# Cross attention whose stacked keys and queries go from SBUF to SBUF in 24 transfers per half batch

## What is computed

```python
qp = q @ Wq.T
kv = latent_kv @ Wkv_expand.T
k, v = jnp.split(kv, 2, axis=-1)
scores = jnp.einsum('bhqd,bhkd->bhqk', qh, kh) * inv_sqrt_d
scores = jnp.where(causal, scores, jnp.finfo(scores.dtype).min)
attn = jax.nn.softmax(scores, axis=-1)
out = jnp.einsum('bhqk,bhkd->bhqd', attn, vh)
return out.transpose(0, 2, 1, 3).reshape(b, sq, H) @ Wout.T
...
x = _layernorm(x + _L0_attn_ref(...), axis=-1)    # a gated convolution
x = _layernorm(x + _L0_xattn_ref(...), axis=-1)   # this part
x = _layernorm(x + _L0_ffn_ref(...), axis=-1)     # a mixture of experts
```

## Time and profile before

| | us |
|---|---|
| profiled execution, its own time | 1183.95 |
| its span | 1182.3 |
| median of the three runs | 1184.79 |
| PE busy | 1076.5 (91%) |
| DVE busy | 683.3 (58%) |
| ACT busy | 457.1 (39%) |
| POOL busy | 284.0 (24%) |

### The profile page before, as it was taken

One profiled execution on the slowest core, in us unless ns is written; L12 is line 12 of the kernel. 1 busy time (PEld: TensorE's weight loads), 2 busy tenths in 40 slices (PEclk: granted clock), 3 DMA queues, 4 the chain that ended last, 5 costly groups with the idle time before them and its releaser, 6 DMA issues. The chain is left out here.

```text
span 1182.3 us, 19299 instructions
## 1 busy us (share of the span) xinstructions
PE 1076.5 (91%) x6850; PEld 910.4 (77%) x6850; DVE 683.3 (58%) x1517; ACT 457.1 (39%) x808; POOL 284.0 (24%) x370
## 2 busy tenths in 40 slices
PE   5999999998758999998868879999999999899996
PEld 4688888887547877886647669899999989777784
DVE  3746375562535666675344747777777767344475
ACT  4613334143324444453334235555555555221210
POOL 4510101006112232333234121111222110223030
PEclk9999999999968999998979889999999999899999
DMA  4402020303878778874243256766666775523141
GB/s 154 167 1 107 0 106 0 106 0 136 236 176 224 189 209 226 216 194 113 73 156 129 78 162 230 248 224 229 224 236 241 227 238 168 178 72 125 53 147 66
DMA packets 88818, 179.31 MB, mean 152 GB/s; under 512 B 8032, under 2 KB 33632, under 8 KB 87104
## 3 DMA queue, kind: packets, MB, share of 16 engines
q1 hardware_dynamic: 82096, 155.06, 42.1%
q0 software_dynamic: 6672, 23.60, 5.9%
HBM read 136.95 MB, written 41.42 MB: 151 GB/s over the span
## 5 line engine op out<-in xcount | busy, mean ns | idle before, releaser
L45 PE MATMUL e_ps_h<-e_x_lo,e_gu_hi 128*128 128x256 f32 (+1 forms) x552 | 155.9, 282 | 5.0 <-DVE e_x_lo L1812 5.0
L46 PE MATMUL e_ps_h<-e_x_hi,e_gu_lo 128*128 128x256 f32 (+1 forms) x552 | 153.8, 279 | 0.0
L47 PE MATMUL e_ps_h<-e_x_hi,e_gu_hi 128*128 128x256 f32 (+1 forms) x552 | 153.6, 278 | 0.0
L804 DVE CUSTOM_DVE_ANT_0 b_dump<-b_ps_s,b_mask 128x128 f32<-128x128 f32 (+1 forms) x256 | 80.1, 354 | 68.6 <-PE b_ps_s L990 67.4
L45 PE MATMUL a_ps_proj<-a_x_lo,arena 128*128 128x512 f32 x256 | 102.4, 400 | 14.9 <-DVE a_x_lo L295 12.1
L45 PEld LDWEIGHTS e_ps_h<-e_x_lo,e_gu_hi 128*128 128x128 f32 (+1 forms) x552 | 99.4, 180 | 6.3 <-DVE e_gu_lo L1816 5.2
L46 PE MATMUL a_ps_proj<-a_x_hi,arena 128*128 128x512 f32 x256 | 101.9, 398 | 0.0
L47 PE MATMUL a_ps_proj<-a_x_hi,arena 128*128 128x512 f32 x256 | 101.8, 398 | 0.0
L309 DVE SCALAR_TENSOR_TENSOR a_xc<-a_ps_proj,a_taps,a_xc 128x510 f32<-128x510 f32 (+2 forms) x96 | 71.6, 746 | 51.2 <-ACT a_xc L268 49.0
L46 PEld LDWEIGHTS e_ps_h<-e_x_hi,e_gu_lo 128*128 128x128 f32 (+1 forms) x552 | 99.5, 180 | 0.9
L47 PEld LDWEIGHTS e_ps_h<-e_x_hi,e_gu_hi 128*128 128x128 f32 (+1 forms) x552 | 99.4, 180 | 0.0
(11 more groups left out here) (306 smaller groups left out, 2699.7 us busy)
## 6 DMA issues: line engine op xcount, KB each, us to landing
f_gate_up_raw<-we_gate_up SPq DMA_DIRECT2D x88, 352.0 KB, 4.7
qk_split<-arena SPq DMA_DIRECT2D x32, 512.0 KB, 6.2
b_sk<-qk_split SPq DMA_DIRECT2D x48, 256.0 KB, 4.1
b_sq<-qk_split SPq DMA_DIRECT2D x48, 256.0 KB, 5.7
f_down_raw<-we_down SPq DMA_DIRECT2D x23, 512.0 KB, 6.7
y_slots<-f_y_tile SPq DMA_DIRECT2D x23, 512.0 KB, 2.8
f_x_next<-x SPq DMA_DIRECT2D x6, 1024.0 KB, 5.7
f_down_raw<-we_down SPq DMA_DIRECT2D x23, 192.0 KB, 6.7
```

The source lines that it names most:

```text
L45: pe.matmul(out, a_hi, b_lo, start=first, stop=False)
L46: pe.matmul(out, a_lo, b_hi, start=False, stop=False)
L47: return pe.matmul(out, a_hi, b_hi, start=False, stop=last)
L804: ins = dve.tensor_tensor_reduce(dump[:, n % 2, cols], ps_s[:, n % 2, cols], mask[:, cols], -1.0, 3e38, ALU.add, ALU.min, peak[:, u, k, i: ...
```

## The change

Three edits, all in `cross_attention`.

1. The DRAM tensor `qk_split`, its stores and the semaphore `split_stored` go. `load_direct` copies from `split` straight into the stacks: for each of three stacked parts and each of the four heads of a chunk one transfer of 32 partitions by 2 by 256 floats (64 KB), 12 for the keys and 12 for the queries of a half. In turns -2 and -1 SP issues the keys and ACT the queries, at fixed places between ACT's activations: batch 0 half 0 after the keys of its half 1; batch 0 half 1 after `fill(-1, 0, 1)`; batch 1 half 0 after `fill(-1, 1, 0)`; batch 1 half 1 after `peaks(0, 0)`, which now stands before the four normalizations. From turn 0 on SP issues both, keys and queries of a half together: half 0 after the residual load, half 1 after the peak rows of batch t+1. The keys' issue carries the wait for batch b-2's last below-peak product of the half. In `keys`, ACT's overwriting of `split` waits for the stack of the batch before instead of its store.
2. `attend` waits for the exponential of head 14 (bank 0 of `ps_x` is free then) and, chunk by chunk, for four more cuts.
3. `normalize` stands in slots (0, 1) and (0, 2), POOL's `rest` in (0, 3) and (0, 4).

```diff
+        def stack_count(b):
+            return 384 * (b + 1)
+        def load_direct(engine, into, parts, b, u):
+            for r, s in enumerate(parts):
+                for h in range(HC):
+                    engine.dma_start(into[r * HD:(r + 1) * HD, b % 2, u, h:UH:HC].bitcast(F32),
+                                     split[h * HD:(h + 1) * HD, u, s].bitcast(F32)).then_inc(stack_loaded[u], 16)
...
         @block.sync
+            def load_keys(b, u):
                 sp.wait_ge(xkq_lo_done, k_count(b, u))
...
                 if b >= 2:
                     sp.wait_ge(e_ready, order(b - 2, u, UH - 1) + 1)
+                load_direct(sp, sk, (KH, KL, KH), b, u)
+            def load_queries(b, u):
+                sp.wait_ge(xkq_lo_done, q_count(b, u))
+                load_direct(sp, sq, (QL, QH, QH), b, u)
...
-                if real(t + 2):
-                    store_k(t + 2, 0)
+                if t < 0:
+                    load_keys(t + 2, 0)
...
-                if real(t + 2):
-                    store_q(t + 2, 0)
-                    load_stack(t + 2, 0)
-                    store_k(t + 2, 1)
+                if t < 0:
+                    load_keys(t + 2, 1)
+                elif real(t + 2):
+                    load_keys(t + 2, 0)
+                    load_queries(t + 2, 0)
                 if real(t + 1):
                     load_peaks(t + 1, 0)
-                if real(t + 2):
-                    store_q(t + 2, 1)
-                    load_stack(t + 2, 1)
+                if t >= 0 and real(t + 2):
+                    load_keys(t + 2, 1)
+                    load_queries(t + 2, 1)
...
         @block.gpsimd
-                        if t and u == 0 and i in (4, 5):
-                            rest(t - 1, i - 4)
+                        if t and u == 0 and i in (3, 4):
+                            rest(t - 1, i - 3)
...
         @block.scalar
                 if b:
-                    act.wait_ge(split_stored, 32 * (2 * (b - 1) + u + 1))
+                    act.wait_ge(stack_loaded[u], stack_count(b - 1))
...
                 if t < 0:
-                    for u in range(2):
-                        for i in range(UH):
-                            fill(t, u, i)
+                    for i in range(UH):
+                        fill(t, 0, i)
+                        if t == -1 and i == 1:
+                            load_queries(0, 1)
+                    fill(t, 1, 0)
+                    load_queries(t + 2, 0)
+                    for i in range(1, UH):
+                        fill(t, 1, i)
                     if t == -1:
+                        peaks(0, 0)
+                        load_queries(1, 1)
                         act.wait_ge(ln_step, TILES + 7)
...
-                        peaks(0, 0)
...
         @block.vector
-                        if t and u == 0 and i in (2, 3):
-                            normalize(t - 1, i - 2)
+                        if t and u == 0 and i in (1, 2):
+                            normalize(t - 1, i - 1)
...
         @block.tensor
-                    pe.wait_ge(stack_loaded[u], 96 * (b + 1))
+                    pe.wait_ge(stack_loaded[u], stack_count(b))
...
             def attend(b):
-                pe.wait_ge(cut_done, HEADS * (b + 1))
+                pe.wait_ge(exp_done, HEADS * (b + 1) - 1)
                 for c in range(DC):
+                    pe.wait_ge(cut_done, HEADS * b + HC * (c + 1))
```

More of the change, by code:

```diff
@@ L384, in __init__, with cross_attention @@
                       (w_o[0], at[2][:, 0:h], at[3][:, 0:h]), (w_o[1], at[2][:, h:n], at[3][:, h:n])]
-def cross_attention(nc, x1_dram, ctx_t, weights, x2_dram, left_ln, ident, xt, c_raw, res, ln, spare, split_dram):
+def cross_attention(nc, x1_dram, ctx_t, weights, x2_dram, left_ln, ident, xt, c_raw, res, ln, spare):
     with ExitStack() as ctx:
@@ L447, in cross_attention @@
         xkq_lo_done = sem("xkq_lo_done")
-        split_stored = sem("split_stored")
         stack_loaded = pair("stack_loaded")
@@ L524, in _ @@
         def _(sp):
-            def store_k(b, u):
+            def load_keys(b, u):
                 sp.wait_ge(xkq_lo_done, k_count(b, u))
[L527 to L538, removed]
                 if b >= 2:
                     sp.wait_ge(e_ready, order(b - 2, u, UH - 1) + 1)
[L541 to L545, removed]
+                load_direct(sp, sk, (KH, KL, KH), b, u)
+            def load_queries(b, u):
+                sp.wait_ge(xkq_lo_done, q_count(b, u))
+                load_direct(sp, sq, (QL, QH, QH), b, u)
             def load_peaks(b, u):
@@ L677, in queries, with load_queries @@
                 act.activation(split[:, u, QH].rearrange("p c t -> p (c t)"), ps_pj[:, 1], ACT.Copy).then_inc(xkq_hi_done, 1)
+            def load_queries(b, u):
+                act.wait_ge(xkq_lo_done, q_count(b, u))
+                load_direct(act, sq, (QL, QH, QH), b, u)
             def peaks(b, u):
@@ L2155, in program @@
     x2 = nc.dram_tensor("x2", (T, D), F32, kind="Internal").ap()
-    split = nc.dram_tensor("qk_split", (2, 4, P, 2 * S), F32R, kind="Internal").ap()
     y = nc.dram_tensor("y_slots", (E_TILES * SLOTS, D), F32, kind="Internal").ap()
@@ L2174, in program @@
             cross_attention(nc, x1, ctx_t, cross, x2_tiles, conv_ln, ident, x_next, ctx_next, sums, ln,
-                            arena[:, 5 * DC * D:], split)
+                            arena[:, 5 * DC * D:])
         rt = Routing(sb)
```

## The result

The changed kernel takes 1229.35 us (median of four runs, 1228.57 to 1232.04) against 1186.69 for the kernel before (four runs); the ratio is 1.038, with a 95% interval of 1.035 to 1.041. It is slower, inside the range of 1178 to 1248 and 9.8 us over the forecast.

What follows compares the result with a forecast made beforehand. PE was taken to bound the steady loop, with SP's issues becoming the bound after the change: 1183.95 + 15.7 (prologue) + 23.9 (loop) - 4 (POOL waits) = 1219.6 us, slower by 3.0%, range 1178 to 1248.

Steps and rivals of the forecast that it cites:

- The issue's price: SP's queue: each new 32-partition transfer costs 0.612 us plus 0.043 to the next, as the stacked loads do.
- cheap rival: SP's queue: issues at a pitch of 0.51 us make the kernel faster, 1174.5 us; break-even at an issue of 0.50; chance 0.18.
- the two-piece store: Existing store to DRAM, two 2 KB pieces a partition, 0.454 us median; the row cited for cheap issues.
- narrowness: DMA issues: few partitions, not bytes or their number, make them dear; 96 or 128 partitions hold SP 0.34 to 0.47 us.
- The loop: Steady batch turns: SP becomes the bound at 37.15 us a turn against PE's 32.35; 23.9 us lost.
- S: Prologue's end: the moment of batch 0's first below-peak product, 339.00 us before, forecast at 354.7.
- The edits on sums and products: Waits of PE for POOL: removing them is worth nothing while SP is the bound, about 4 us back at the end.
- The prologue: Before the loop: ACT's blocks of 12 issues delay normalizations, then SP's keys and peak rows; 15.7 us lost.
- the dear one at 0.745: SP's queue: issues cost as the peak rows do; prologue loses 20.7 us, loop 46.7, total 1247; chance 0.10.
- The transfers themselves: Copies: a narrow path over the same 32 partitions makes them late, whatever the issue; counted within the forecast, no separate chance.
- Queues that hinder each other: Prologue: ACT and SP take turns issuing, two stretches cost another 7.9 us each, total 1235; chance 0.23.
- the DRAM path as hidden: Steady loop before the change: stacked loads busy the DMA engines 0.82 of the turn but don't hold up PE.

Runs made afterwards that it cites:

- run 4: Changed kernel, from batch 2 on one 96-partition transfer replacing three of 32 (same bytes, contents other than the layout needs): 1178.18 us, ratio 0.994.
- run 7: Changed kernel plus bursts of SBUF-to-SBUF copies of several widths behind its end; total not compared, SP issues 0.593 us at 32 partitions, 0.630 at 128.
- run 2: Changed kernel without the edits to sums, normalization and POOL's rest, so direct stacking alone: 1232.12 us, ratio 1.038 to the kernel before.
- run 5: Changed kernel with SP, in turn -1, issuing batch 1's second keys and the peak rows before waiting for the normalizations: 1218.2 us, ratio 1.027.
- run 9: Changed kernel with four 96-partition transfers for twelve of 32 everywhere, prologue included (contents other than the layout needs): 1161.15 us, ratio 0.978.
- run 3: Changed kernel, from batch 2 on each stacked transfer moving one chunk instead of two, as many issues: 1224.61 us, ratio 1.033.
- run 1: Kernel before, stacks through DRAM, with only the sums waiting per four cuts and normalization and POOL's rest one slot sooner: 1177.01 us, ratio 0.991.
- run 6: Kernel before with earlier sums, normalization and rest, and SP's turn -1 normalization wait moved behind batch 1's second-half loads: 1174.91 us, ratio 0.989.
- run 8: Kernel of run 6, but from batch 2 on keys go direct from SBUF to SBUF, queries still through DRAM: 1162.77 us, ratio 0.981.
- run 10: Changed kernel plus bursts of DRAM stores, DRAM loads and SBUF copies behind its end; total not compared, one-piece loads 0.421 to 0.432 us.

## Why the prediction was right, and where by luck

**The issue's price.** Taken as 0.612 + 0.043; measured 0.597 + 0.042. The cheap rival's break-even, an issue of 0.50, was not reached: its witness, the two-piece store, was the wrong neighbour. But so was my argument for the other. I said that the price goes with narrowness; runs 4 and 7 show 0.63 us at 96 and 128 partitions. The rule would have called the 96-wide form cheap. A row on record spoke against it: the x2 store covers 128 partitions and holds SP for 0.602 us in the median, outside the 0.34 to 0.47 us that I gave for wide transfers. And the 0.338 of the 96-row load is that of an issue standing alone, where the new ones stand in blocks of 24. The safe half of the reasoning was to take the row that has the new transfer's own pieces and partitions, and not to reason from it.

**The loop, forecast 23.9 us lost, measured 29.8.** SP is the bound, as the turn above shows. The 5.9 us between the two are:
- Turn 0 began its first 24 issues 4.3 us later than I had it, and at the end of turn 1 SP was 4.6 us late. I opened them with slot 7 (S+10.8), but SP's turn begins with the peak rows of half 1, which left at 368.61 (S+11.8), and x, context and two residual loads follow; the first key left at 371.96, S+15.1. I had listed that order for every later turn and left it out of the first.
- The four turns took 150.4 us against 148.6. The x2 store landed after 3.0 us (3.8 estimated), and with the residual that gives back 0.7 in the turn shown; but its 24 issues took 16.2 and 16.7 us instead of 15.7. That is mostly single long issues: of 288 in the loop, 11 took more than 0.9 us, up to 1.74, together 9.6 us over the median. That is why a block of 12 takes 7.6 to 7.8 us or, in most other cases, 8.3 to 9.1.
- From the last x2 store to the second half of turn 6 it took 3.5 us, 0.6 less than allowed.

The long issues are not spread by chance. The page lists a queue that brings instructions, 30 transfers of 16 KB in this execution:

```profile
q8 instruction: 30, 0.49, 0.2%
```

By the start times of the trace's DMA records 10 of the 11 long issues begin 0.01 to 0.55 us after such a transfer does, and 11 of 11 in run 2; 14 of these transfers start while SP issues the loop's stacks. Only the one at 372.68 has none. No run takes these transfers away, so that they cause the long issues is not shown.

**The edits on sums and products.** Worth at most little inside the loop: right (run 2; there SP goes from its first key of the loop to its last x2 store in 223.5 us without them and 222.5 with them). The 4 us at its end came back only in part. From the second half of turn 6 to the first matmul of the next phase, busy time of the kernel before, the changed one, run 2 (without the edits) and run 4 (with them, and a third of the issues):

```profile
550.33:602.78 52.45, 41.55 (x405) 32.07 (x405) 19.46 (x63) 17.90 (x40) 15.78 (x31) 0.93 0.13 42
```

```profile
597.93:648.75 50.82, 43.19 (x404) 33.62 (x405) 17.90 (x54) 17.53 (x39) 15.29 (x30) 0.89 0.16 53
```

```profile
599.03:653.80 54.77, 44.06 (x405) 33.77 (x405) 17.90 (x54) 17.49 (x39) 15.35 (x30) 0.88 0.15 50
```

```profile
548.95:596.57 47.62, 39.79 (x405) 30.90 (x405) 19.46 (x63) 17.89 (x40) 15.71 (x31) 0.96 0.16 53
```

The waits behaved: PE's idle time falls by 3.3 us, from 10.90 to 7.63, and run 2 has 10.71 of it again. The stretch is 4.0 us shorter in the changed kernel than in run 2, so as a price of the edits the 4 us were right. What the sum left out is PE's clock. After turns 2 to 5, in which it idled 4.5 to 6.8 us each, PE is granted 0.89 here, a mean of stretches at 2.4 GHz and at 1.2, and is busy for 43.19 us; in run 4, whose turns 2 to 5 have at most 1.0 us of idle time, the same 405 matmuls take 39.79 us at 0.96, with the same edits and nearly the same idle time. So the lower clock costs 3.4 us beside run 4 and 1.6 beside the kernel before (0.93), and 1.6 of the 4 us came. In the loop the clock is lower too (0.91 in the turn shown, 0.87 in the next, 1.00 before) and costs nothing, since SP sets the pace. These are single profiled executions; the other 1.4 us that came back lie in the later phases, which vary by as much from run to run.

**The prologue, forecast 15.7, measured 16.6** (17.8 less the 1.2 with which the phase began). The walk held step by step: blocks ended on ACT at 307.50, 317.81, 330.06 and 342.04, against 305.5, 316.0, 327.5 and 340.1. Runs 5 and 9 show its two causes.

**The rivals.** The cheap issue is out (run 7), and so is the dear one at 0.745. The transfers themselves: out (runs 3 and 4). Queues that hinder each other: the rows decide. While SP issued keys, ACT's 12 took 9.05 and 8.48 us; nearly alone, 7.73 and 7.75. If the two took turns, 12 would last 15.7. They didn't: both issue at nearly full rate side by side, and in the first of these stretches one long issue on each queue at the same moment (1847 ns on SP, 1507 on ACT, near 301 us) makes up most of the rest; a transfer of the instruction queue starts there at 301.0. SP has such blocks of 8.4 us alone too (345.44). The Trainium skill, "Perfetto Trace Analysis", section "DMA Instruction — HWDGE (DVE, Sync)", says that the block which writes descriptors is locked for one sequencer at a time. As a halving of the rate when both issue, which is how I had read it, this trace disagrees; a shared stall now and then is all that it shows.

**What the forecast didn't see.** It took the DRAM path as hidden and the queue as the only question. Runs 1 and 6 show that without the POOL waits what comes by way of DRAM, and the peak rows behind it in the queue, is late too. The real choice was between a path with little room and a queue with none, and a mixture of the two beats both (run 8).

## What to carry to other kernels

Before splitting transfers, add up the issues that one queue must make in a period of the bound, at the measured 0.6 us each with the gap (0.64): here 48 of them are 31 us of a 30 us period, whatever they carry and however fast they land. An issue on ACT's queue costs ACT the same 0.6 us, in front of whatever stands behind it, so a block of 12 between activations is a stall of 7.7 us. Where one path is late and the other fills the queue, try a split: keys direct and queries through DRAM took the 0.989 of run 6 to 0.981, and a direct path for all lost 3.8%. And an engine that is made to wait can pay again later: PE's lower clock after the loop cost 3.4 us beside run 4.

## What the runs showed of the hardware

- A DMA issue's price depends on its form and hardly on its size or width: 0.59 to 0.65 us from 32 to 128 partitions SBUF to SBUF (runs 4 and 7), 0.591 with half the bytes (run 3); 0.42 to 0.43 for a load from DRAM in one piece a partition (run 10).
- It also depends on what stands before it: the same context load holds SP for 0.33 us alone and 0.43 right behind another issue, the x2 store for 0.38 and 0.60.
- SP and ACT issue side by side at 0.60 and 0.62 us each.
- Now and then an issue takes 0.9 to 1.8 us, once on both queues at the same moment. In the changed kernel 10 of the loop's 11 such issues begin within 0.6 us after a 16 KB transfer of the instruction queue begins, in run 2 all 11. That the one causes the other is not shown.
- 64 KB from SBUF to SBUF land 2.0 us after the start of the issue; four transfers for twelve, 192 KB each, in 4.1.
- The same 405 matmuls at the end of cross attention keep PE busy for 39.79 us at a granted clock of 0.96 (run 4) and for 43.19 at 0.89 (the changed kernel, where PE idled 4.5 to 6.8 us in each turn before).
